# Layer 0's scores and rough pieces run as 64-row halves of the array, and VectorE makes the low parts of phi and v

## What is computed

```python
# layer 0 (inner width 64)
g_x     = einsum('ic,bcn->bni', g_w, xf) + g_b
theta_x = einsum('ic,bcn->bni', theta_w, xf) + theta_b
phi_x   = einsum('ic,bcn->bin', phi_w, xf) + phi_b
y = softmax(einsum('bni,bim->bnm', theta_x, phi_x)) @ g_x
x = einsum('ci,bin->bcn', W_w, y^T) + W_b + xf
# layer 1 (width 128)
q, k, v = projections of x by Wq, Wk, Wv (128 x 128) with their biases
out = softmax(q k / sqrt(128)) @ v
x = x + out^T
```

## Time and profile before

| | |
|---|---|
| time, median of 3 runs | 3431.91 us (3431.13 to 3433.36) |
| the profiled execution, span | 3433.7 us |
| PE busy | 3336.5 us (97%) |
| POOL busy | 2965.9 us (86%) |
| DVE busy | 2100.6 us (61%) |
| ACT busy | 1671.5 us (49%) |
| chain that ended last, PE's share | 91% |
| groups L398 (pieces from phi and from k), PE busy | 361.4 and 345.4 us |
| granted TensorE clock, mean | 0.989 |

### The profile page before, as it was taken

The page is one execution under the profiler, slowest core; times in us unless marked ns, Lnnn a source line. Parts: engine busy times, 40 slices in busy tenths (PEclk is TensorE's granted clock), DMA queues, the critical chain, the costliest instruction groups (busy, mean ns, idle before and its releaser), DMA issues.

```text
span 3433.7 us, 46684 instructions
## 1 busy us (share of the span) xinstructions
PE 3336.5 (97%) x13124; PEld 2113.4 (62%) x13124; DVE 2100.6 (61%) x3029; ACT 1671.5 (49%) x2241; POOL 2965.9 (86%) x1366
## 2 busy tenths in 40 slices
PE   6999999999999989999999998999999999999998
PEld 4555566666655556666655555666665555566665
DVE  4555576776555557676755555677675555666674
ACT  4455445444455544444445554544454555444444
POOL 4999699898989969898989996989898999688897
PEclk9999999999999999999999999999999999999999
DMA  1000000000000000000000000000000000000000
GB/s 43 13 18 19 28 10 22 12 22 16 19 19 16 19 23 16 16 19 19 13 19 19 19 16 23 19 13 21 16 19 13 19 19 16 19 13 16 13 13 10
DMA packets 34038, 61.73 MB, mean 18 GB/s; under 512 B 5280, under 2 KB 5920, under 8 KB 33568
## 3 DMA queue, kind: packets, MB, share of 16 engines
q1 hardware_dynamic: 33824, 59.23, 5.6%
HBM read 42.44 MB, written 16.78 MB: 17 GB/s over the span
## 4 chain that ended last, share of the span: by engine, by line
PE 91%; DVE 3%; issue 2%; POOL 2%; ACT 1%; SPq 0%; DVEq 0%; DMA 0%; ACTq 0%; POOLq 0%
PE acc_out L471 16%; PE rough L398 15%; PE acc_out L455 13%; PE scores L420 7%; PE scores L423 7%; PE scores L425 7%; PE scores L429 7%; PE scores L426 7%; PE acc_out L443 2%; PE acc_out L441 2%; PE acc_out L442 2%; DVE piece_max L793 2%; PE rough L380 2%; PE acc_out L492 1%; PE acc_out L386 1%
## 5 line engine op out<-in xcount | busy, mean ns | idle before, releaser
L280 POOL TENSOR_TENSOR sums<-sums,probs 128x1024 f32<-128x1024 f32 x886 | 2116.0, 2388 | 145.1 <-ACT probs L718 104.7
L793 DVE TENSOR_REDUCE piece_max<-rough 128x1 f32<-128x512 f32 x2024 | 1309.5, 684 | 649.1 <-PE rough L398 646.2
L810 DVE TENSOR_TENSOR probs<-scores,shift_rows 128x1024 f32<-128x1024 f32 x512 | 626.7, 1224 | 567.3 <-PE scores L429 543.2
L718 ACT ACTIVATE probs<-scores 128x1024 f32<-128x1024 f32 x512 | 520.1, 1025 | 672.8 <-PE scores L423 665.1
L711 ACT ACTIVATE probs<-probs 128x1024 f32<-128x1024 f32 x512 | 539.4, 1053 | 499.6 <-DVE probs L810 499.4
L914 POOL TENSOR_TENSOR p_lo<-probs,p_hi 128x1024 fp32r<-128x1024 f32 x192 | 459.2, 2392 | 188.0 <-ACT probs L711 187.7
L471 PE MATMUL acc_out<-probs,v_vals 128*128 128x512 f32 x1280 | 605.4, 595 | 0.0
L425 PE MATMUL scores<-qry_a,k_hi 128*128 128x512 f32 x1024 | 507.8, 496 | 0.0
L455 PE MATMUL acc_out<-probs,g_vals 128*64 128x512 f32 x2048 | 495.0, 605 | 0.0
L420 PE MATMUL scores<-qry_a,phi_a 128*128 128x512 f32 x1024 | 432.3, 422 | 0.0
L710 ACT ACTIVATE p_hi<-probs 128x1024 fp32r<-128x1024 f32 x192 | 203.3, 1059 | 441.0 <-DVE probs L810 397.2
(11 more groups left out here) (97 smaller groups left out, 2961.0 us busy)
## 6 DMA issues: line engine op xcount, KB each, us to landing
x_q<-x SPq DMA_DIRECT2D x32, 256.0 KB, 2.7
x_res<-x SPq DMA_DIRECT2D x32, 256.0 KB, 3.0
mid<-mid_new SPq DMA_DIRECT2D x32, 256.0 KB, 2.2
x_q<-mid SPq DMA_DIRECT2D x32, 256.0 KB, 2.7
x_res<-mid SPq DMA_DIRECT2D x32, 256.0 KB, 3.2
out<-result SPq DMA_DIRECT2D x32, 256.0 KB, 2.3
x_kv<-x SPq DMA_DIRECT2D x24, 256.0 KB, 2.7
probs<-x SPq DMA_DIRECT2D x2, 1024.0 KB, 6.0
```

What stands on the lines that cost most here:

```text
L280: eng.tensor_tensor(sums[:, parity], sums[:, parity], probs[:, s % P_BUFS], ALU.add).then_inc(s_plus, 1)
L793: nc.vector.reduce_max(piece_max[:, t, c:c + 1], src, AX.X).then_inc(s_reduced, 1)
L810: nc.vector.tensor_tensor(probs[:, s % P_BUFS].rearrange("p (h c) -> p h c", c=QB), scores[:, s % 2].rearrange("p (h c) -> p h c", c=QB), ...
```

## The change

The two halves of the array's rows are used as arrays of their own. `phi_a` and `phi_b` go; `phi_hi` and `phi_lo` take their place, each 128 x 2048: key tiles with even number lie in rows 0 to 63, those with odd number in rows 64 to 127. Scores of layer 0 are four terms for each key tile (high x high, low x high, high x low, 1/64 x shift row), each a matmul over 64 rows, issued in turn for the two halves. Rough pieces for layer 0 become pairs: two matmuls over 64 rows into the two banks of `rough`, then one VectorE maximum over 128 x 2 x 512 into two columns. A block that prepares a block of layer 0 has 16 pairs (PAIRS), one in each of the groups 0 to 13 and a second in 8 and 12 (`PAIRS_AT`); a pair waits until the pair before it is reduced. Blocks that prepare layer 1 keep single pieces (`PIECES_AT`, `TURN_PIECES_AT`). The shift row is copied to `shift_rows` in both layers. `take_phi` is two copies of 64 x 256; the low parts of phi (`phi_low`, group 11) and of v (`v_low`, group 14) are made by VectorE, reading PSUM; `split_phi` and `split_v` leave GpSimd. g is projected at group 12.

```diff
-PIECES_AT = [[3 if s in three else 2 if s < 14 else 0 for s in range(16)]
-             for three in ((7, 8, 11, 13), (7, 8, 10, 12))]
+PIECES_AT = [3 if s in (7, 8, 10, 12) else 2 if s < 14 else 0 for s in range(16)]
+PAIRS_AT = [[2 if s in two else 1 if s < 14 else 0 for s in range(16)] for two in ((8, 12), (8, 12))]
-PHI_AT, G_AT = 9, 11
+PHI_AT, G_AT = 9, 12
+PHI_LO_AT = 11
...
+        rough_pair = rough[:].rearrange("p (h c) -> p h c", c=QB)
+        pair_banks = (rough_pair, acc_out[:])
...
+            def rough_of_pair(parity, pair, places):
+                t, c = pair
+                for h in range(TPG):
+                    last = mm(places[:, h], qry_a[half(h), parity, t * P:(t + 1) * P], cols(phi_hi, c)[half(h)],
+                              start=True, stop=True)
+                last.then_inc(s_rough, 1)
...
+                if layer == 0:
+                    k = slice(s * KT, (s + 1) * KT)
+                    for n, (keys, qry) in enumerate(((phi_hi[:, k], qa), (phi_lo[:, k], qa), (phi_hi[:, k], qb),
+                                                     (share[:], shift_rows[:, parity]))):
+                        if s == 0 and n == 2:
+                            pe.wait_ge(l_q, g + 1)
+                        if s == 0 and n == 3:
+                            pe.wait_ge(s_row_sb, g + 1)
+                        for h in range(TPG):
+                            last = mm(scores[:, s % 2, h * QB:(h + 1) * QB], keys[half(h)], qry[half(h)],
+                                      start=n == 0, stop=n == 3)
+                    last.then_inc(s_scores, 1)
+                    return
...
+            def first_pairs(c):
+                if c == 0:
+                    pe.wait_ge(h_q, 1)
+                pe.wait_ge(h_phi, 2 * c + 2)
+                for m in range(c * SUB, (c + 1) * SUB):
+                    if m >= 2:
+                        pe.wait_ge(s_reduced, m)
+                    rough_of_pair(0, pairs[m], pair_banks[m % 2])
             for c in range(BLOCKS):
                 if c >= 2:
-                    pe.wait_ge(h_phi, c - 1)
+                    pe.wait_ge(l_phi, c)
...
+                    if by_pair:
+                        pe.wait_ge(s_reduced, st.rough + m + 1)
+                        rough_of_pair(1 - st.parity, pairs[m], rough_pair)
+                    else:
+                        pe.wait_ge(s_reduced, st.rough + max(m, 1))
+                        rough_piece(1 - st.parity, pieces[m], two_banks(m))
...
-                copy(whole[0:IC], src[0:IC], PHI_B[0:IC])
-                copy(cols(phi_b, c)[IC:P], src[IC:P], PHI_B[IC:P])
-                copy(cols(phi_a, c), src, PHI_B).then_inc(h_phi, 1)
+                for h in range(TPG):
+                    last = copy(half_tiles(phi_hi, h, c), tiles_of_half(src, h), PHI_B[half(h)])
+                last.then_inc(h_phi, 1)
...
+            def reduce_pair(n, pair, src):
+                t, c = pair
+                dve.wait_ge(s_rough, n + 1)
+                nc.vector.reduce_max(piece_max[:, t, TPG * c:TPG * (c + 1)], src, AX.X).then_inc(s_reduced, 1)
+
+            def phi_low(n, c, src):
+                dve.wait_ge(h_phi, n + 1)
+                for h in range(TPG):
+                    last = nc.vector.scalar_tensor_tensor(
+                        out=half_tiles(phi_lo, h, c), in0=tiles_of_half(src, h), scalar=PHI_B[half(h)],
+                        in1=rd(half_tiles(phi_hi, h, c)), op0=ALU.add, op1=ALU.subtract)
+                last.then_inc(l_phi, 1)
+
+            def v_low(n, c, src):
+                dve.wait_ge(h_v, n + 1)
+                at = bass.ds(c, 1) if not isinstance(c, int) else slice(c, c + 1)
+                nc.vector.tensor_tensor(v_lo[:, at], src[:, TPG * KT:].unsqueeze(1), rd(v_hi[:, at]),
+                                        ALU.subtract).then_inc(l_v, 1)
```

More of the change, by code:

```diff
@@ L50, with __init__ @@
 class Step:
-    def __init__(self, layer, b, i, i_known, prev, nxt, more, blocks, pieces_per_block):
+    def __init__(self, layer, b, i, i_known, prev, nxt, more, blocks, pairs, pieces):
         self.layer, self.b, self.i, self.prev, self.nxt = layer, b, i, prev, nxt
@@ L85, in build @@
     PIECES = SUB * BLOCKS
[L86 removed]
+    HALF = N // 2
+    PAIRS = PIECES // 2
+    assert GROUPS == len(PIECES_AT) and sum(PIECES_AT) == PIECES == sum(TURN_PIECES_AT) + SUB
+    assert all(GROUPS == len(a) and sum(a) == PAIRS for a in PAIRS_AT)
     assert BLOCKS == 8 and LAG == 3
@@ L94, in build @@
     last_pieces = pieces[-SUB:]
+    pairs = [(t, c) for c in range(BLOCKS // 2) for t in range(SUB)]
     with ExitStack() as ctx:
@@ L418, in score_group @@
                     place = scores[:, s % 2, h * QB:(h + 1) * QB]
[L419 to L429, removed]
+                    mm(place, k_hi[:, k], qa, start=True, stop=False)
+                    mm(place, k_lo[:, k], qa, start=False, stop=False)
+                    if s == 0 and h == 0:
+                        pe.wait_ge(l_q, g + 1)
+                    last = mm(place, k_hi[:, k], qb, start=False, stop=True)
                 last.then_inc(s_scores, 1)
@@ L536, in _ @@
             pe.wait_ge(h_g, BLOCKS)
+            pe.wait_ge(l_phi, BLOCKS + 1)
             def block_program(st):
-                at = TURN_PIECES_AT if st.turn else PIECES_AT[st.layer]
+                by_pair = st.nxt == 0
+                at = PAIRS_AT[st.layer] if by_pair else TURN_PIECES_AT if st.turn else PIECES_AT
+                most = 1 if by_pair else 2
                 free_bank = acc_out[:, 1 - st.parity]
@@ L544, in piece @@
                     nonlocal m
-                    t, c = pieces[m]
+                    t, c = pairs[m] if by_pair else pieces[m]
                     if m == 0:
@@ L863, in _, with reduce @@
             dve.wait_ge(s_vec, 2)
-            for m, piece in enumerate(pieces):
-                reduce_piece(m, piece, four_banks[m % SUB])
-            shift(0, 0)
+            for c in range(BLOCKS):
+                phi_low(c, c, scores[:, c % 2, 0:QB])
+                if c % 2 == 1:
+                    for m in range((c // 2) * SUB, (c // 2 + 1) * SUB):
+                        reduce_pair(m, pairs[m], pair_banks[m % 2])
+            shift(0, 0, PAIRS)
             def block_program(st):
-                at = TURN_PIECES_AT if st.turn else PIECES_AT[st.layer]
+                by_pair = st.nxt == 0
+                at = PAIRS_AT[st.layer] if by_pair else TURN_PIECES_AT if st.turn else PIECES_AT
+                most = 1 if by_pair else 2
+                free_bank = acc_out[:, 1 - st.parity]
                 m = 0
+                def reduce():
+                    nonlocal m
+                    if by_pair:
+                        reduce_pair(st.rough + m, pairs[m], rough_pair)
+                    else:
+                        reduce_piece(st.rough + m, pieces[m], two_banks(m))
+                    m += 1
                 for s in range(GROUPS):
@@ L886, in block_program @@
                     if st.nxt is not None:
[L887 to L892, removed]
+                        for _ in range(at[s]):
+                            reduce()
                 if st.ends:
```

122 lines of the change are left out of this document (58 added, 64 removed).

## The result

The changed kernel takes 3445.76 us, median of 4 runs (3445.42 to 3448.51), against 3431.75 us before: ratio 1.0044 with a 95% interval of 1.0031 to 1.0056. It is slower by 14.0 us; the forecast was 13.7.

The account below looks back on a forecast made before the run. PE was taken to bound both layers' blocks. Pieces -114.6, changes of shape +86, new waits +71.9, old waits -30.2, first stage +0.6 sum to +13.7 us: 3445 us, range 3375 to 3500.

Parts of the forecast that it names:

- The step of 0.231 us: Scores and pairs: two half-row matmuls together take 0.231 us, so scores cost 0 and halved pieces save 114.6 us.
- a shorter step (0.215): Rival for the half-row steps: 0.016 us less in each of 2544, 40 us less, 3405 us; chance 0.10.
- a longer one (0.25): Rival for the half-row steps: two loads and two matmuls issued take 0.25 us, 48 us more, 3493 us; chance 0.12.
- halves in series: Rival: the row halves don't run together; score steps cost 473 us more, pairs another 115, 4033 us; chance 0.05.
- The 3.07 of four row tiles: Skill page's speedup, read as a step of 1.3 in place of 1, adding 178 us; counted to the longer-step rival's tail.
- The changes between rows and whole: PE switching between half rows and whole array: 430 changes at 0.20 us, +86 us; 9 in a regular block, 1.8 us.
- The rival of cheap changes: Changes between rows and whole array cost little: 3402 us at half price, 3359 at none; chance 0.28.
- The waits: PE waiting for VectorE's pair reductions: 0.66 us four times in a regular block, +71.9 us against -30.2 for old waits.
- The moved parts: Low parts of v and phi moved to VectorE: hidden, cost 0, with 7 us as the other end.
- The last block of layer 0: Scores in halves, 28 pieces for layer 1 whole: 19 changes each, block about 3.8 us longer.
- Block 0 behind layer 1: Layer 0's first block in images after the first: 13 changes at 0.20 us and three waits, 1.98 us.
- The first image's stage: VectorE's 16 reductions and 8 low parts of phi replace GpSimd's link: +0.6 us, between -3 and +4.

Follow-up runs that it names:

- e7: Changed kernel with both halves of each rough pair run over rows 0 to 63: 3558.1 us, ratio 1.0365 to the kernel before.
- e2: Changed kernel with layer 0's small operations, shift row excepted, on rows 0 to 63 alone, other rows' sums left out: 3407.62 us, ratio 0.9926 to the kernel before.
- e9: Changed kernel with two pairs moved to avoid waits and layer 0's next-query projection put beside the shift row, whole computation kept: 3398.5 us, ratio 0.9900 to before.
- e6: Changed kernel with the low part of v in the blocks given back to GpSimd: 3447.3 us, ratio 1.0041 to the kernel before.
- e1: Changed kernel with VectorE's pair maximum reading only half of each bank, the rest left out: 3371.64 us, ratio 0.9818 to the kernel before.

## Why the prediction was right, point by point

**The step of 0.231 us** held: the starts after are 0.23 apart. The rivals of a shorter step (0.215), a longer one (0.25) and of halves in series are out; e7 shows what series would cost for the pairs alone, 112 us against 115 worked out. The 3.07 of four row tiles, in the Trainium skill's page "TensorE: Matmul & The Clock Gate", Part 3, has no counterpart here: two row halves gave 2.0 (0.23 for two).

**The changes between rows and whole** cost 0.40 us for two at the output projection, as priced. Taking 209 of them away gave 38 us in e2 where 42 less 4 for waits were expected, and in e9 two fewer in a block gave 0.39 us where 0.40 was expected. The rival of cheap changes, 0.28 of the chances, is out. The Trainium skill's page "TensorEngine Tiling (Array Packing)", section "Tiling Modes", says that a change of mode drains the engine. The traces agree in so far as each change costs time, for rows (0.20 us each) as for columns (0.34 a round trip).

The blocks that no experiment takes changes from agree as well: layer 1's last block, 32 changes more and 32 pieces made into 16 pairs, grew by 2.8 us, where the prices give 6.4 - 3.7 = 2.7.

**The waits** have their worked-out distance, 1.82 us from pair to pair, and the reduction its 1.22. The block came out at 43.76, worked out 43.7.

**The moved parts** are hidden, as said: e6 for v, the unchanged 59.9 us of layer 1 for phi.

**Sizes that were off.** The last block of layer 0 grew by 3.5, not 3.8 (4 blocks: 1.2 us). Of before's four the first, at 62.8 us, spent 10 us at 1.2 GHz and the others, at 63.6 to 63.8, 14 us, as all four after did; against its like the growth is 3.3. Block 0 behind layer 1 gained 0.53, not 0.2. The first image's stage lost 1.5 in these two traces, where I had 0.6; by the spread above the traces can't tell the two figures apart. Of the others none moves the sum by more than 1.2 us. That the sum agrees with the table (13.6) and with the timed runs (14.0) to 0.3 us is luck: the parts but the stage are right to about a us each, the stage is open by a few, and my own range for waits and small terms was 3432 to 3459. In e1 that stage gained 8.4 where I had said 5.

**What I missed.** I read the 1.8 us between the profiled span of before and the median as if the execution were ordinary, and forecast a span of 3447.4. The span after is 3443.6, and its own time 3445.42: a time is about 1.8 us *above* its span, in nearly all of the timed executions. The profiled execution of before was some 3.8 us long for its kernel, by the stretch at the lower clock shown above, and my comparison of span and median hid that. The forecast of the median was right since it was built as a difference.

## What to carry to other kernels

Here splitting the array paid for what it removed (112 us for the pairs, e7) and charged 0.20 us at each border: count the changes of shape in the instruction order, price them from a change that the trace already has, and put work of one shape side by side before you split. When two small results become one with no second buffer, the consumer's time plus both latencies becomes a distance that the producer must cover with other work; read that distance from one wait in the old trace, and place the pieces by it. With both done, the same idea that lost 0.4% gains 1.0%.

## What the runs showed of the hardware that I had not expected

With both matmuls of a pair on rows 0 to 63 (e7), matmuls on rows 64 to 127 that stand later in the program start first. The timeline of PE in e7, with pair and scores of one group:

```profile
205.29 0.39 PE L435 MATMUL rough<-phi_hi,qry_a 64*128 64x512 f32 x1
205.31 0.39 PE L464 MATMUL scores<-qry_a,phi_hi 64*128 64x512 f32 x1
205.53 0.39 PE L435 MATMUL rough<-phi_hi,qry_a 64*128 64x512 f32 x1
205.55 0.39 PE L464 MATMUL scores<-qry_a,phi_lo 64*128 64x512 f32 x1
...
206.01 0.39 PE L464 MATMUL scores<-shift_rows,share 64*128 64x512 f32 x1
...
206.46 0.39 PE L464 MATMUL scores<-shift_rows,share 64*128 64x512 f32 x1
```

The score matmul at 205.31 comes behind both pair matmuls in the program, and runs 0.22 us ahead of the second. In this place the two halves of the rows run as two queues. So they do in e2 above, where scores start beside the output projection (208.53) and ahead of its second pass (208.97), though they stand behind it in the program. The last score matmul of the program's order (the second half, which carries the signal) starts at 206.01, the first half's last one at 206.46, and ScalarE reads both at 206.97:

```profile
206.97 1.02 ACT L767 ACTIVATE probs<-scores 128x1024 f32<-128x1024 f32 x1 [0.35 <-PE scores L464]
```

0.51 us after the later start, the same distance as in the group before it in that trace. So here the signal waited for the matmuls ahead of it in the program although its own work was done 0.45 us earlier. One place shows that, and it is not proved as a rule.
